# Softmax denominators from sums over four key tiles instead of two, in the first attention of a fused two-layer kernel

## The reference, cut to what matters

```
q = concat(q_c, q_r); k = concat(k_c, k_r)          # 128 + 32 wide
scores = einsum('bhsd,bhtd->bhst', q, k) * scale    # 1024 x 1024
attn = softmax(scores, axis=-1)                     # exp(s - max) / sum over t of exp(s - max)
o = einsum('bhst,bhtd->bhsd', attn, v_c)
```

## Time and profile before

| | |
|---|---|
| median of three runs | 840.13 us |
| profiled execution, its time | 839.71 us |
| its span | 838.0 us |
| first attention, units 0 to 7 | 56.90 to 332.89 us of the span |
| TensorE busy over the span | 771.7 us (92%) |
| VectorE | 614.8 us (73%) |
| ScalarE | 509.5 us (61%) |
| GpSimd | 402.2 us (48%) |

### The profile page before, as it was taken

One profiled execution on the slowest core, in us unless ns is written; L12 is line 12 of the kernel. 1 busy time (PEld: TensorE's weight loads), 2 busy tenths in 40 slices (PEclk: granted clock), 3 DMA queues, 4 the chain that ended last, 5 costly groups with the idle time before them and its releaser, 6 DMA issues.

```text
span 838.0 us, 13880 instructions
## 1 busy us (share of the span) xinstructions
PE 771.7 (92%) x4612; PEld 452.1 (54%) x4612; DVE 614.8 (73%) x1615; ACT 509.5 (61%) x866; POOL 402.2 (48%) x461
## 2 busy tenths in 40 slices
PE   5899999999999988999999989799999999999986
PEld 2454444444454433589888865455555555564544
DVE  5897678786777798865247678887777778787554
ACT  3346666756657576356556466467776687776762
POOL 3506776676766683707070685847444122220121
PEclk9999999999999999999999999899999999999998
DMA  9300000000000000123121030000000000000001
GB/s 345 149 28 0 1 2 0 1 1 1 1 1 1 2 1 1 51 67 123 64 86 51 26 102 14 23 4 1 1 1 1 1 2 1 1 1 1 1 1 51
DMA packets 14540, 25.35 MB, mean 30 GB/s; under 512 B 3175, under 2 KB 9193, under 8 KB 14345
## 3 DMA queue, kind: packets, MB, share of 16 engines
q1 hardware_dynamic: 11798, 18.85, 6.5%
q0 software_dynamic: 2048, 4.20, 1.6%
q10 hardware_dynamic: 626, 1.43, 0.5%
HBM read 15.03 MB, written 9.44 MB: 29 GB/s over the span
## 4 chain that ended last, share of the span: by engine, by line
PE 39%; DVE 16%; issue 3%; ACT 2%; POOL 2%; DMA 0%; ACTq 0%; DVEq 0%; POOLq 0%
PE ps L1683 7%; PE ps L1768 6%; PE ps L1748 4%; DVE ps L2549 4%; PE ps L1654 3%; DVE mx_part L2552 3%; PE ps L1636 2%; PE ps L1638 2%; PE ps L1646 2%; PE ps L1637 2%; PE ps L1601 1%; PE ps L1549 1%; PE ps L1565 1%; PE ps L1776 1%; ACT pt L1112 1%
## 5 line engine op out<-in xcount | busy, mean ns | idle before, releaser
L2062 DVE TENSOR_REDUCE mx_part<-ps 128x1 f32<-128x512 f32 x256 | 163.6, 682 | 54.6 <-PE ps L1327 53.7
L1112 ACT ACTIVATE pt<-ps 128x1024 f32<-128x1024 f32 (+1 forms) x160 | 149.7, 938 | 72.1 <-PE ps L1748 71.0
L905 ACT ACTIVATE pt<-ps 128x512 f32<-128x512 f32 x256 | 140.9, 596 | 70.3 <-PE ps L1353 63.3
L1683 PE MATMUL ps<-rounded 128*128 128x128 f32 (+2 forms) x352 | 124.9, 388 | 14.7 <-DVE mx_part L2552 4.8
L2549 DVE CUSTOM_DVE_ANT_0 ps<-ps,wm 128x128 f32<-128x128 f32 (+3 forms) x256 | 119.6, 518 | 18.9 <-PE ps L1683 17.3
L1353 PE MATMUL ps<-rounded 100*128 100x512 f32 x256 | 120.7, 484 | 10.6 <-ACT pt L905 9.8
L857 ACT ACTIVATE rounded<-ps 128x512 fp32r<-128x512 f32 (+3 forms) x160 | 94.4, 592 | 56.2 <-PE ps L1315 20.1
L723 POOL TENSOR_SCALAR_AFFINE_SELECT pt<-pt 128x512 f32<-128x512 f32 x64 | 39.9, 635 | 172.5 <-ACT pt L1112 172.4
L1748 PE MATMUL ps<-rounded 128*128 128x512 f32 (+2 forms) x352 | 115.3, 368 | 0.0
L1327 PE MATMUL ps<-rounded 98*128 98x512 f32 x266 | 103.7, 413 | 2.2 <-DVE mx_part L2062 1.3
L2552 DVE TENSOR_REDUCE mx_part<-ps 128x1 f32<-128x512 f32 x128 | 82.4, 686 | 27.7 <-PE ps L1683 27.6
(11 more groups left out here) (308 smaller groups left out, 1289.4 us busy)
## 6 DMA issues: line engine op xcount, KB each, us to landing
wm<-in_wm SPq DMA_DIRECT2D x1, 4896.0 KB, 15.8
to_experts<-kstage SPq DMA_DIRECT2D x6, 512.0 KB, 4.6
of_experts<-pt SPq DMA_DIRECT2D x12, 256.0 KB, 2.0
kstage<-to_experts SPq DMA_DIRECT2D x10, 256.0 KB, 2.8
wm<-in_experts SPq DMA_DIRECT2D x1, 1540.0 KB, 7.5
x<-in_x SPq DMA_DIRECT2D x4, 256.0 KB, 5.9
out<-x SPq DMA_DIRECT2D x4, 256.0 KB, 2.3
early<-in_wo ACTq DMA_DIRECT2D x1, 512.0 KB
```

What stands on the lines that cost most here:

```text
L905: nc.scalar.activation(pt0(k, i), ps[:, ST0_BANKS[i % 2], :], ACT.Exp, scale=SCALE0).then_inc(exp_done, 1)
L1112: nc.scalar.activation(pt[:, 4 * (t % 2) + 2 * g:4 * (t % 2) + 2 * g + 2, 0:w], ps[:, ST1_BANKS[2 * g]:ST1_BANKS[2 * g] + 2, 0:w], ACT.Exp ...
L1683: ins = mm(bank[:, o:o + w], queries1(u, i), keys[:, 0:w], start=(o == 0), stop=(o == parts[-1][1]))
L2062: v.tensor_reduce(mx_part[u % 2][:, o:o + 1], ps[:, max_bank(u, n), :], AX_X, ALU.max).then_inc(max_done, 1)
```

## The change

In units 0 to 6 the sums over two key tiles are added once more, in pairs, to sums over four tiles: `quad_adds(u, q)`, q = 0, 1 (NQSUM = 2). Of the four pieces GpSimd adds two and VectorE two, in place, in the buffer of the first. The denominators then take two groups of matmuls in a unit: that of q = 0 behind the values of step 6, and that of q = 1 behind the values of step 2 of the next unit. The buffers of `sums` are used in the order 0, 1, 1, 0. New semaphores `quad_pool` and `quad_dve` count the new sums; the pair sums of j = 0 and j = 2 wait for both, those of j = 1 and j = 3 for denominators. Unit 7 keeps its four groups.

GpSimd's new sums of q = 0 stand behind the products of the unit before and in front of `low_max`; those of q = 1 behind the pair sums of j = 3. VectorE's of q = 1 stand in the next unit between the maxima of steps 0 and 1, those of q = 0 behind the last correction of step 4, in front of the maxima of step 5. VectorE's reciprocals are moved later, between the maxima of steps 2 and 3.

```diff
--- before.py
+++ after.py
@@ -56,7 +56,7 @@
 UH = H0 // HP
 QH = S // CH
 HQ = HP * QH
-NPAIR = TS // 2
+NPAIR, NQSUM = TS // 2, TS // 4
 SCALE0 = 1.0 / float(DK + DR) ** 0.5
 
 E0, F0 = 8, 352
@@ -135,7 +135,7 @@
 Z0_FIRST = 2
 Z0_AT = {1: (1, 3), 3: (2, 0), 4: (2, 1)}
 TURN0_AT = {(5, 1): 0, (6, 0): 1, (6, 1): 2, (7, 0): 3}
-DEN0_AT, DEN0_LAST_AT = {3: 0, 5: 1, 7: 2}, {4: 0, 5: 1, 7: 2}
+DEN0_AT, DEN0_LAST_AT = {6: 0}, {4: 0, 5: 1, 7: 2}
 
 
 
@@ -372,6 +372,7 @@
         prep_mm, prep_done = sem("prep_mm"), sem("prep_done")
         cq_mm, cq_hi, cq_lo, kv_mm, kv_done, ckv_mm, ckv_done = map(
             sem, ("cq_mm", "cq_hi", "cq_lo", "kv_mm", "kv_done", "ckv_mm", "ckv_done"))
+        quad_pool, quad_dve = map(sem, ("quad_pool", "quad_dve"))
         cq_copied, ctx_T, rden_ok, pair_add, den_mm, bias_add = map(sem, ("rden_ok", "cq_copied", "ctx_T", "pair_add", "den_mm", "bias_add"))
         v_copied, ctx1_T, ctx1_turn = map(sem, ("v_copied", "ctx1_T", "ctx1_turn"))
         v_ones = sem("v_ones")
@@ -422,7 +423,8 @@
             return pt[:, HQ * (k % 2) + i, :]
 
         def sums(u, j):
-            return pair_sum[j % 2 + (2 if u >= SUMS_MOVE else 0)]
+            k = (0, 1, 1, 0)[j] if u + 1 < U0 else j % 2
+            return pair_sum[k + (2 if u >= SUMS_MOVE else 0)]
 
         def half_rows(u, c):
             r0 = HP * DC * ((c + u) % 2)
@@ -582,11 +584,21 @@
                 G = u * NPAIR + j
                 for i in range(HQ):
                     pool.wait_ge(exp_done, (u * TS + 2 * j + 1) * HQ + i + 1)
-                    if i == 0 and G >= 2:
-                        pool.wait_ge(den_mm, G - 1)
+                    if i == 0 and (u or j > 1):
+                        if j % 2:
+                            pool.wait_ge(den_mm, u * NQSUM + (1 if j == 3 else 0))
+                        else:
+                            pool.wait_ge(quad_pool, HP * (u * NQSUM + j // 2))
+                            pool.wait_ge(quad_dve, HP * (u * NQSUM + j // 2))
                     if i == 0 and u == SUMS_MOVE and j == 0:
                         pool.wait_ge(z_mm, 4 * U0)
                     nc.gpsimd.tensor_tensor(sums(u, j)[i], pt0(0, i), pt0(1, i), ALU.add).then_inc(pair_add, 1)
+
+            def quad_adds(u, q):
+                pool.wait_ge(pair_add, (u * NPAIR + 2 * q + 2) * HQ)
+                for i in range(HP):
+                    a, b = (sums(u, 2 * q + k)[i] for k in range(2))
+                    nc.gpsimd.tensor_tensor(a, a, b, ALU.add).then_inc(quad_pool, 1)
 
             def early_low_weights():
                 for n, e in enumerate(EARLY_EXPERTS):
@@ -624,6 +636,8 @@
                         early_low_weights()
                     if u and j == 1:
                         contexts_out(u - 1)
+                    if j % 2 and u + 1 < U0:
+                        quad_adds(u, j // 2)
                     if j == 1 and u + 1 < U0:
                         low_max(u + 1)
                     if u == 0:
@@ -667,7 +681,7 @@
             nc.gpsimd.memset(first_stack[:, 0:HG, :].bitcast(F32), 0.0).then_inc(first_zero, 1)
             scatter(1)
             pool.wait_ge(prep_mm, 4)
-            pool.wait_ge(den_mm, U0 * NPAIR)
+            pool.wait_ge(den_mm, (U0 - 1) * NQSUM + NPAIR)
             nc.gpsimd.memset(v1[:, :, :, :, DH:DH + 1], 1.0).then_inc(v_ones, 1)
             gather(0)
             gather(1)
@@ -1364,9 +1378,15 @@
             def denominators(u, pp, j):
                 if j == 0 and u:
                     pe.wait_ge(rden_ok, 4 * u)
-                pe.wait_ge(pair_add, (u * NPAIR + j + 1) * HQ)
+                last = NQSUM - 1 if u + 1 < U0 else NPAIR - 1
+                if u + 1 < U0:
+                    pe.wait_ge(quad_pool, HP * (u * NQSUM + j + 1))
+                    pe.wait_ge(quad_dve, HP * (u * NQSUM + j + 1))
+                else:
+                    pe.wait_ge(pair_add, (u * NPAIR + j + 1) * HQ)
                 for i in range(HQ):
-                    ins = mm(ps[ctx_rows(pp, i), DEN_BANK, :], ones[:, 0:DC], sums(u, j)[i], start=(j == 0), stop=(j == NPAIR - 1))
+                    ins = mm(ps[ctx_rows(pp, i), DEN_BANK, :], ones[:, 0:DC], sums(u, 2 * j if u + 1 < U0 else j)[i],
+                             start=(j == 0), stop=(j == last))
                 ins.then_inc(den_mm, 1)
 
             def o_mms(c):
@@ -1439,8 +1459,8 @@
                         values(u, pp, k - 1)
                     elif u:
                         values(u - 1, 1 - pp, TS - 1)
-                    if k == 1 and u:
-                        denominators(u - 1, 1 - pp, NPAIR - 1)
+                    if k == 2 and u:
+                        denominators(u - 1, 1 - pp, NQSUM - 1)
                     den_at = DEN0_AT if u + 1 < U0 else DEN0_LAST_AT
                     if k in den_at:
                         denominators(u, pp, den_at[k])
@@ -2078,11 +2098,17 @@
 
             def context_rden(u, q):
                 if q == 0:
-                    dve.wait_ge(den_mm, (u + 1) * NPAIR)
+                    dve.wait_ge(den_mm, (u + 1) * NQSUM if u + 1 < U0 else u * NQSUM + NPAIR)
                     if u:
                         dve.wait_ge(ctx_out, QH * u)
                 cols = slice(q * P, (q + 1) * P)
                 v.reciprocal(cT[:, 0, cols], ps[:, DEN_BANK, cols]).then_inc(rden_ok, 1)
+
+            def quad_adds(u, q):
+                dve.wait_ge(pair_add, (u * NPAIR + 2 * q + 2) * HQ)
+                for i in range(HP, HQ):
+                    a, b = (sums(u, 2 * q + k)[i] for k in range(2))
+                    v.tensor_tensor(a, a, b, ALU.add).then_inc(quad_dve, 1)
 
             def last_sums(j):
                 u = U0 - 1
@@ -2090,7 +2116,11 @@
                     dve.wait_ge(exp_done, (u * TS + 2 * j + 1) * HQ + i + 1)
                     if i == 0:
                         dve.wait_ge(pair_add, (u * NPAIR + j) * HQ)
-                        dve.wait_ge(den_mm, u * NPAIR + j - 1)
+                        if j == 0:
+                            dve.wait_ge(quad_pool, HP * u * NQSUM)
+                            dve.wait_ge(quad_dve, HP * u * NQSUM)
+                        else:
+                            dve.wait_ge(den_mm, u * NQSUM + j - 1)
                     v.tensor_tensor(sums(u, j)[i], pt0(0, i), pt0(1, i), ALU.add).then_inc(pair_add, 1)
 
             def last_context(u):
@@ -2145,22 +2175,28 @@
                 if u + 1 < U0:
                     z_lo_part(u + 1, 1 - u % 2, Z0_FIRST)
                 pieces(0, 2, 3, 4)
+                if u:
+                    quad_adds(u - 1, 1)
                 pieces(1, 0, 1, 2, 3, 4)
+                z_lo_at(1)
+                pieces(2, 0, 1, 2)
                 rden(0)
-                z_lo_at(1)
+                pieces(2, 3, 4)
                 rden(1)
-                pieces(2, 0)
-                rden(2)
-                pieces(2, 1, 2, 3, 4)
-                rden(3)
                 if (u, 2) in OUT_AT:
                     add_output1(OUT_AT[u, 2])
-                pieces(3, 0, 1, 2, 3, 4)
+                pieces(3, 0)
+                rden(2)
+                pieces(3, 1, 2)
+                rden(3)
+                pieces(3, 3, 4)
                 z_lo_at(3)
                 pieces(4, 0, 1, 2, 3, 4)
                 if u + 1 < U0:
                     split_max(u + 1)
                 z_lo_at(4)
+                if u + 1 < U0:
+                    quad_adds(u, 0)
                 for k in range(5, TS):
                     pieces(k, 0, 1, 2, 3, 4)
                     if u == U0 - 3 and k < 7:
@@ -2169,7 +2205,8 @@
                     second_stats(TC, TS)
                     half_var(1, 0)
                     quick_rstd(0)
-                    dve.wait_ge(den_mm, SUMS_MOVE * NPAIR - 1)
+                    dve.wait_ge(quad_pool, HP * SUMS_MOVE * NQSUM)
+                    dve.wait_ge(quad_dve, HP * SUMS_MOVE * NQSUM)
                     for c in range(QH):
                         norm_chunk(c)
```

## The result

The kernel after takes 860.82 us (median, 857.20 to 861.46), the kernel before beside it 839.99: ratio 1.024 (95% interval 1.021 to 1.028). The prediction was 840.9, in a range from 833.5 to 845.5: the measured time is 15 us above its upper end. The profiled execution took 860.17 us, with a span of 858.4 against 838.0.

A forecast was written before the change was run, and what follows sets the result against it. TensorE was taken to set the pace. Unit 0 -1.9, units 1 to 5 +0.2 +0.2 -0.1 -0.1 +0.5, the end +2.0: +0.8 us on a span of 838.0, giving a median of 840.9 us, range 833.5 to 845.5.

The forecast's parts named there:

- Removed: TensorE, units 0 to 6: four denominator groups become two, 0.85 us each, 11.9 us in all at most.
- Unit 2: Followed step by step: VectorE's new sums at 23.0 to 25.25, step 5's last maxima tile at 25.95, unit 0.2 us longer.
- Units 1 to 5: Sum over these units of the first attention: 0.7 us longer in all.
- All that steps 3 and 5 gave, 1.9 us, is lost here: Step 5 of unit 2: TensorE's last maxima tile waits for VectorE, coming at 25.95 against 25.76 before.
- Unit 1 is as unit 2: Unit 1 of the first attention: 0.2 us longer, like the unit after it.
- no wait: Step 1, worked out for unit 2: TensorE writes the last maxima tile at 7.2, its bank read by 6.95.
- Unit 5: Sixteen output matmuls at step 2 put everything later; VectorE's new sums end at 258.7, unit 0.5 us longer.
- units 3 and 4: They copy queries on GpSimd; some time returns with step 7's group gone: 0.1 us shorter each.
- Unit 0: No products or reciprocals: 1.0 us gained at step 5, 0.9 from step 7's group, 1.9 shorter in all.
- +2.0 together with unit 6's 0.7: Units 6 and 7: the last exponential waiting for VectorE's sums comes 2.0 us later, including unit 6 ending 0.7 later.
- with GpSimd held off all along: Unit 7: VectorE's casts 1.82, two new sums 1.3, four sums 2.6 us run without GpSimd between, ending at 315.7.
- Rival (c): Units 6 and 7: VectorE is passed over by GpSimd's runs, +6 us at the end instead of +2, 845; chance 0.20.

The follow-up runs named there:

- e1: The change without any of the new sums or the waits for them, half of the denominators' terms missing: 830.62 us, ratio 0.988.
- e2: The change without VectorE's new sums, GpSimd's kept, the terms of two pieces missing: 841.83 us, ratio 1.002.
- e3: The change without GpSimd's new sums, VectorE's kept, the terms of two pieces missing: 841.42 us, ratio 1.003.
- e6: The change in units 0 to 5 alone, with VectorE's sums of q = 0 two maxima later, on another chip: ratio 1.004.
- e4: The complete change, with the third tile for the maxima of step 5 computed seven times in units 0 to 5: 853.72 us, ratio 1.017.
- e11: The change in unit 6 alone; units 0 to 5 keep four groups of sums over two tiles: 851.74 us, ratio 1.015.
- e8: The complete change, with GpSimd's low weights in unit 7 moved behind the products of unit 6, on another chip: ratio 1.025.
- e9: The change in units 0 to 5, a third sum buffer, VectorE's q = 0 sums before step 6's maxima, their denominators at step 7: 862.61 us, ratio 1.030.

## Why the prediction was wrong

**Removed: right.** e1's units 1 and 2 are 1.6 shorter, where two groups of 0.85 are 1.7.

**Unit 2: right.** 22.98, 25.23 and 26.11 against 23.0, 25.25 and 25.95; unit 2 is 0.4 longer against 0.2. The cause, VectorE's sums in front of p(5,0) with GpSimd's beside them, is shown by e2, e3 and e6.

**Units 1 to 5 (0.7 predicted, 10.5 measured): the step that failed is "All that steps 3 and 5 gave, 1.9 us, is lost here".** I priced the stand at its own length. A stand of 1.6 to 1.7 us in an otherwise full stretch was followed by a granted clock of half in four of five units, for 3.4 us and in unit 1 for 6.8, which cost 7.8 us; e4 gives just that back. The remaining 2.7 against 0.7 has a second failed step, "Unit 1 is as unit 2": unit 1 takes 1.5 more than before even with the clock held (36.53), where I had 0.2. The pair of q = 1 that I took to be clean meets GpSimd's bias there and takes 2.49 us instead of 1.3, and p(1,3), for which I had "no wait", waits 0.93. Unit 5 takes 0.9 more where I had 0.5; units 3 and 4 are 0.1 and 0.0 shorter, as forecast.

**Unit 0 (-1.9 predicted, -1.3 measured)**: right sign, a third too large; why isn't traced.

**Units 6 and 7 (2.0 predicted, 12.7 measured): the term "+2.0 together with unit 6's 0.7" was mis-sized.** Unit 6 lost 1.8: 0.8 with the clock held (e4), and the rest by the fall behind its stand of 2.22 us. For unit 7 I took VectorE's sums at their undisturbed 0.65, "with GpSimd held off all along". They took 2.07 each: the two engines alternated. The prediction reads eight sums as running beside the low parts, of which one took 2.18; in the trace only four did (308.2 to 313.7, the other four at 324), so it was one in four. Rival (c) named the passing over, with the small step's 3.78 us for it; I priced it at 4 more and left out the clock again. An estimate for the 11.0 us that unit 7 lost: TensorE waits 3.6 us more than before (6.7 for the exponentials against 3.1), and a granted clock of 0.81 over 44 us is up to 8.4 us. No run holds the clock in unit 7, so the split is not shown. e11 shows that unit 6's sums alone do this, e2 and e3 that either engine's are enough, e8 that 3.6 us of it go when the four low weights don't run beside VectorE's sums.

The Trainium skill, page "SBUF — State Buffer", section "Who interferes with whom", says that issue order decides who blocks, and for whole instructions. Unit 7 agrees: four VectorE sums and four GpSimd instructions in turn, 8.28 and 7.97 us. In e9 one VectorE sum waited through all that was left of four GpSimd sums (4.20 us, 1.25 each), so there it was not turn and turn about, and the case doesn't show what decides between the two.

## What to carry to other kernels

A stand of the engine that sets the pace can cost two to three times its length (here 1.7 us of standing, and 1.6 or 3.1 us more by the clock): look for the granted clock behind it, and count the time at half of it. The same stand may be followed by a fall in one unit and not in the next, so compare units in which it fell with units in which it didn't. Before adding work to a helper that is nearly full, list what it hands on, one after another; here the maxima, the pair sums and the exponentials each took over the wait that was removed from the one before. Where VectorE and GpSimd both read SBUF, price a sum by the run of instructions on the other side, not by its own length, and don't lift a wait that happens to keep them apart.

## What the runs showed that I had not expected

- Six superfluous matmuls in each of units 0 to 5 made the kernel 7 us faster (853.72 beside 860.82), through the granted clock.
- One VectorE sum of 0.65 us took 4.20 beside four GpSimd sums in a row, and 1.29 for two with a wait in front of them.
- Four casts of weights, 1.82 us before, took 5.89 us beside GpSimd's low parts (e2), and 6.28 (e11) and 5.12 (e8) beside its pair sums and new sums.
